# A fused two-layer transformer kernel: the first pages of its third expert run are chosen by their number and released by a count made on the chip, not sorted by a page map

## What is computed

```python
x = x + 0.5 * _L0_ffn_ref(_layernorm(x), ...)    # run 0: 8 experts of width 176, top 2, and a shared expert
x = x + _L0_attn_ref(_layernorm(x), ...)         # time shift, gates, a channel mix of 1024 hidden units
x = x + 0.5 * _L0_ffn_ref(_layernorm(x), ...)    # run 1: the weights of run 0 again
x = x + 0.5 * _L1_ffn_ref(_layernorm(x), ...)    # run 2: 32 experts of width 96, top 6, and a shared expert
x = x + _L1_attn_ref(_layernorm(x), ...)         # rotary q and k, one sum over the sequence, projection
x = x + 0.5 * _L1_ffn_ref(_layernorm(x), ...)    # run 3: the weights of run 2 again
```

```python
scores = sigmoid(x @ gate_w);  topk_w, topk_i = top_k(scores, 6);  topk_w /= sum(topk_w) + 1e-20
routed = sum over the 6 chosen experts e of  topk_w * ((silu(x @ wg[e]) * (x @ wu[e])) @ wd[e])
out    = routed + (silu(x @ sg) * (x @ su)) @ sd
```

## Time and profile before

| | us |
|---|---|
| median of 3 runs (lowest, highest) | 1299.98 (1296.2, 1301.84) |
| the profiled execution's own time | 1301.21 |
| its span, first to last instruction | 1299.4 |
| PE busy in the span | 1110.7 (85%) |
| DVE busy | 746.4 (57%) |
| ACT busy | 536.0 (41%) |
| POOL busy | 594.8 (46%) |
| third run's tile loop, PE | 712.12 to 914.06 |
| fourth run's tile loop, PE's first page | 1107.10 |

### The profile page before, as it was taken

One profiled execution on the slowest core, in us unless ns is written; L12 is line 12 of the kernel. 1 busy time (PEld: TensorE's weight loads), 2 busy tenths in 40 slices (PEclk: granted clock), 3 DMA queues, 4 the chain that ended last, 5 costly groups with the idle time before them and its releaser, 6 DMA issues. The chain is left out here.

```text
span 1299.4 us, 20577 instructions
## 1 busy us (share of the span) xinstructions
PE 1110.7 (85%) x6035; PEld 918.2 (71%) x6035; DVE 746.4 (57%) x2345; ACT 536.0 (41%) x1012; POOL 594.8 (46%) x579
## 2 busy tenths in 40 slices
PE   4899997887898999988687899999968674899994
PEld 3777775566677887766565799988545553899994
DVE  4663365645635574366645564777788655545554
ACT  3423344464533432244441344444242324466663
POOL 3580244221213233237767303667536777017776
PEclk9799998999988999999888999999888887899998
DMA  9623535920000236534353767887302232569997
GB/s 315 281 94 90 154 102 166 323 98 1 1 1 33 87 141 257 201 120 144 127 198 129 234 209 218 282 252 226 92 8 81 102 106 101 176 205 285 295 288 239
DMA packets 126073, 209.84 MB, mean 161 GB/s; under 512 B 16064, under 2 KB 105536, under 8 KB 124096
## 3 DMA queue, kind: packets, MB, share of 16 engines
q1 hardware_dynamic: 101392, 141.38, 32.8%
q0 software_dynamic: 24576, 67.14, 16.6%
HBM read 129.29 MB, written 101.19 MB: 177 GB/s over the span
## 5 line engine op out<-in xcount | busy, mean ns | idle before, releaser
L713 POOL DMA_INDIRECT G<-yd,slot_of x256 | 251.1, 981 | 297.9 <-DMA yd<-yo 216.4
L698 POOL DMA_INDIRECT xd<-xnt,slot_of x256 | 251.6, 983 | 152.4 <-issue 78.7
L982 PE MATMUL ps<-WE,xT 128*128 x1016 | 190.0, 331 | 0.6 <-issue 0.2
L2210 DVE TENSOR_TENSOR hid<-hid,ps 128x192 f32<-128x192 f32 (+2 forms) x168 | 65.3, 389 | 180.9 <-ACT hid L1624 180.6
L982 PEld LDWEIGHTS ps<-WE,xT 128*128 128x128 f32 x1016 | 164.7, 193 | 2.7 <-issue 2.6
L2189 DVE SCALAR_TENSOR_TENSOR XT<-G,wt,XT 128x256 f32<-128x256 f32 x256 | 127.6, 503 | 62.1 <-DMA G<-yd,slot_of 52.9
L1595 ACT ACTIVATE xT<-ps 128x512 f32<-128x512 f32 (+1 forms) x168 | 99.0, 589 | 140.4 <-PE ps L949 134.6
L1624 ACT ACTIVATE hid<-ps 128x192 f32<-128x192 f32 (+2 forms) x168 | 60.3, 359 | 164.3 <-PE ps L982 164.3
L949 PE MATMUL ps<-ident,xd_in 128*128 128x128 f32 x664 | 102.5, 276 | 29.7 <-DMA xd_in<-xd 20.7
L949 PEld LDWEIGHTS ps<-ident,xd_in 128*128 128x128 f32 x664 | 81.5, 142 | 42.9 <-issue 23.3
L1452 ACT ACTIVATE S<-ps 128x512 f32<-128x512 f32 (+1 forms) x72 | 42.6, 592 | 159.7 <-PE ps L887 157.4
(11 more groups left out here) (265 smaller groups left out, 2168.4 us busy)
## 6 DMA issues: line engine op xcount, KB each, us to landing
xd_in<-xd SPq DMA_DIRECT2D x140, 256.0 KB
yd<-yo SPq DMA_DIRECT2D x140, 256.0 KB, 3.2
WE<-w SPq DMA_DIRECT2D x8, 1280.0 KB, 10.2
xd_in<-xd SPq DMA_DIRECT2D x52, 128.0 KB, 2.3
yd<-yo SPq DMA_DIRECT2D x52, 128.0 KB, 2.0
W0E<-w0e SPq DMA_DIRECT2D x1, 4864.0 KB, 33.3
xd<-xnt,slot_of POOLq DMA_INDIRECT x256, 2.4
G<-yd,slot_of POOLq DMA_INDIRECT x256, 4.1
```

The lines of the kernel that those rows point to most:

```text
L698: nc.gpsimd.indirect_dma_start(xd[f // 2][:, :], bass.IndirectOffsetOnAxis(ap=slot_of[:, t, k:k + 1], axis=0), xnt[:, t, :], None).then_in ...
L713: nc.gpsimd.indirect_dma_start(G[:, n % G_RING, :], None, yd[f // 2][0:min(ly.upto[t][k], ly.TILES) * P, :], bass.IndirectOffsetOnAxis(ap= ...
L982: last = mm(dst, xT[:, q % 2, a, k, :], flat[:, bass.ds(expert[2 * q + a] + k * 2 * ly.H, 2 * ly.H)], start=(k == 0), stop=(k == KD - 1))
L2210: tt(hid[:, q % 2, 0:m, 0:ly.H], hid[:, q % 2, 0:m, 0:ly.H], src, ALU.mult).then_inc(TL.hid, 1)
```

## The change

The page map goes, with the per-page DMAs and their second semaphores, `page_order`, `omap` and the third gather in every fourth pair. Pages keep their numbers. FRONT becomes 20: after block 2 DVE still marks the whole pages, and after block 3 is ranked PE counts the whole ones ahead of each page. Partition 20 then holds how many of pages 0 to 19 are whole. If that is under 20, `more_rows` becomes 96, else 0. SP reads it into a register and waits for each of the four scatter semaphores to reach the count of blocks 0 to 2 plus this number, where 96 more stands for the 24 scatters of block 3. So the first ten pairs are loaded either as soon as blocks 0 to 2 are scattered and block 3's slots are known, or after the whole scatter. SP no longer waits for `emap`. Before pair 10 it waits for the whole scatter, as it did before pair 8. The attention weights follow the load of pair 10. Gathers wait for the pairs of `pages(t, k)` alone: 16 pairs at the least. Steps of `first_turns` are at other pairs.

```diff
-FRONT = [0, 0, 16, 0]
+FRONT = [0, 0, 20, 0]
...
-        self.upto = [[pages(t, k) for k in range(top)] for t in range(TT)]
-    def early(self, front):
-        moved = lambda n: max(n, front + min(n, self.E)) if front else n
-        return [[-(-moved(n) // 2) for n in row] for row in self.upto]
+        self.early = [[-(-pages(t, k) // 2) for k in range(top)] for t in range(TT)]
...
                 def send(q):
...
-                    if moved(q):
-                        if moved_upto(q, q % 2):
-                            wait_tile(sp, tile_sent, q, q % 2)
-                        for a, done in enumerate((TL.sent[q % Y_RING], tile_sent[q % 2][0])):
-                            sp.dma_start(yd[f // 2][bass.ds(page_at[2 * q + a], P), :], yo[:, q % Y_RING, a]).then_inc(done, 16)
-                        return
                     sp.dma_start(pairs_of(yd[f // 2])[q - q0][:, 0:m], yo[:, q % Y_RING, 0:m]).then_inc(TL.sent[q % Y_RING], 16)
-                scattered_upto(sp, GATHER0[f] + (NB - 1 if FRONT[f] else NB) * ly.NG)
                 if FRONT[f]:
-                    sp.wait_ge(RT.emap, f + 1)
+                    sp.wait_ge(RT.slots, NB * f + NB)
+                    left = sp.value_load(more_rows[FRONT[f]:FRONT[f] + 1, 0:1], min_val=0, max_val=16 * ly.NG // IN_FLIGHT)
+                    for n in range(IN_FLIGHT):
+                        sp.wait_ge(scattered[n], left + 16 * len(range(n, GATHER0[f] + (NB - 1) * ly.NG, IN_FLIGHT)))
+                else:
+                    scattered_upto(sp, GATHER0[f] + NB * ly.NG)
...
-                    if moved(q) and i % 2 == 0:
-                        next_pages(f, q)
-                    if moved(q):
...
-                        for a, done in enumerate((TL.landed[q % X_RING], tile_landed[q % 2][0])):
-                            sp.dma_start(xd_in[:, q % X_RING, a], xd[f // 2][bass.ds(page_at[2 * q + a], P), :]).then_inc(done, 16)
-                    else:
...
+                    sp.dma_start(xd_in[:, q % X_RING, 0:m], pairs_of(xd[f // 2])[i][:, 0:m]).then_inc(TL.landed[q % X_RING], 16)
...
             def attention_weights(i):
-                if i == 3:
+                if i == 10:
...
-                if t in (4, 8, 12):
-                    inverse(AT_NORM, (t - 4) // 4)
+                if t in (5, 9, 13):
+                    inverse(AT_NORM, (t - 5) // 4)
...
                 if b == NB - 1 and FRONT[f]:
-                    before(f, bank)
+                    mm(ps[:, bank, 3 * P:3 * P + 2], tri[:, :], whole_page[:, :].broadcast_to([P, 2]), start=True, stop=True)
...
                 dve.wait_ge(RT.ranked, NB * f + b + 1)
+                if b == NB - 1 and FRONT[f]:
+                    st.do(ts(more_rows[:, :], ps[:, bank, 3 * P:3 * P + 1], float(FRONT[f]), 16.0 * ly.NG / IN_FLIGHT, ALU.is_lt, ALU.mult))
...
-                    for _ in range(per_pair + (1 if FRONT[f] and (q - q0) % 4 == 3 else 0)):
+                    for _ in range(per_pair):
...
-                page_order(2, route_banks(NB - 1)[1])
```

More of the change, by code:

```diff
@@ L188, in program @@
         ecol = sb("ecol", [P, 16], F32)
-        page_map = sb("page_map", [P, P], I32)
-        emap, omap = page_map[0:1, :], page_map[32:33, :]
+        emap = sb("emap", [1, P], I32)
         whole_page = sb("whole_page", [P, 1], F32R)
-        order = sb("order", [P, 6], F32)
+        still_open = sb("still_open", [P, 1], F32)
+        more_rows = sb("more_rows", [P, 1], I32)
         wt = sb("wt", [P, TT, 8], F32)
@@ L498, in pairs_of @@
             return dram.rearrange("(n a p) d -> n p a d", a=2, p=P)
[L500 to L514, removed]
         def sent_upto(eng, n):
@@ L559, in _ @@
             sp.dma_start(WSQ[:], wsq).then_inc(wsq_in, 16)
[L561 to L569, removed]
             def tiles(f, between=None):
@@ L848, in rank @@
                 mm(ps[:, bank, (2 * NT - 1) * E:2 * NT * E], ones, half(E), start=False, stop=True).then_inc(RT.ranked, 1)
-            def before(f, bank):
-                mm(ps[:, bank, 2 * P:3 * P], ones, tri[:, :], start=True, stop=True)
-                mm(ps[:, bank, 3 * P:3 * P + 2], tri[:, :], whole_page[:, :].broadcast_to([P, 2]), start=True, stop=True)
             def expert_row(f, bank):
                 pe.wait_ge(RT.ecol, f + 1)
-                places = ident[:, :]
-                if FRONT[f]:
-                    places = eq[0][:, :, :].rearrange("p t e -> p (t e)")
-                    mm(ps[0:1, bank, 2 * P:3 * P], cvec[:, 0:1], places, start=True, stop=True)
                 if f == 3:
-                    mm(ps[0:1, bank, P:2 * P], ecol[:, 14:15], places, start=True, stop=True)
-                mm(ps[0:1, bank, 0:P], ecol[:, 13:14], places, start=True, stop=True).then_inc(RT.erow, 1)
+                    mm(ps[0:1, bank, P:2 * P], ecol[:, 14:15], ident[:, :], start=True, stop=True)
+                mm(ps[0:1, bank, 0:P], ecol[:, 13:14], ident[:, :], start=True, stop=True).then_inc(RT.erow, 1)
             def gate_up(ch, ahead):
@@ L943, in turned @@
                     pe.wait_ge(TL.landed[q % X_RING], 16 * (q // X_RING + 1))
-                    if moved(q):
-                        wait_tile(pe, tile_landed, q + 1, q % 2)
                     pe.wait_ge(TL.xT, q)
@@ L1609, in finished @@
                     if q >= Y_RING:
-                        sent_before(act, q)
+                        act.wait_ge(TL.sent[q % Y_RING], 16 * (q // Y_RING))
                     m = ly.tiles_in(q - q0)
@@ L2011, in whole_pages @@
                 st.sync()
-                st.do(ts(here, opens, cvec[:, 0:1], 0.0, ALU.is_equal, ALU.add, accum_out=order[:, 0:1]))
+                st.do(ts(here, opens, cvec[:, 0:1], 0.0, ALU.is_equal, ALU.add, accum_out=still_open[:, :]))
                 st.sync()
-                st.do(stt(whole_page[:, :], pages[:, :], cvec[:, 0:1], order[:, 0:1], ALU.is_gt, ALU.subtract))
-            def page_order(f, bank):
-                column = lambda i: order[:, i:i + 1]
-                ahead, n = ps[:, bank, 3 * P:3 * P + 1], float(FRONT[f])
-                st.sync()
-                taken, front, behind, apart_by, place = (column(i) for i in range(1, 6))
-                st.do(ts(taken, ahead, n, None, ALU.min))
-                st.do(stt(front, ahead, n, whole_page[:, :].bitcast(F32), ALU.is_lt, ALU.mult))
-                st.sync()
-                st.do(stt(behind, taken, -1.0, cvec[:, 0:1], ALU.mult, ALU.add))
-                st.sync()
-                st.do(stt(apart_by, ahead, -n, behind, ALU.add, ALU.subtract))
-                st.sync()
-                st.do(stt(place, apart_by, front, behind, ALU.mult, ALU.add))
-                st.sync()
-                ts(eq[0][:, :, :].rearrange("p t e -> p (t e)"), ps[:, bank, 2 * P:3 * P], place, n, ALU.subtract, ALU.is_equal).then_inc(RT.ecol, 1)
+                st.do(stt(whole_page[:, :], pages[:, :], cvec[:, 0:1], still_open[:, :], ALU.is_gt, ALU.subtract))
             def slots(f, b, bank):
@@ L2110, in slots @@
                         st.sync()
[L2111 to L2115 removed]
+                    ts(ecol[:, 13:14], ecol[:, 12:13], float(ly.EW), None, ALU.mult).then_inc(RT.ecol, 1)
             def experts(f, bank):
@@ L2214, in rows @@
                     if q >= Y_RING:
-                        sent_before(dve, q)
+                        dve.wait_ge(TL.sent[q % Y_RING], 16 * (q // Y_RING))
                     m = ly.tiles_in(q - q0)
@@ L2243, in tiles @@
                         weight_pair(f, n // rounds, 2 * (n % rounds))
-                    for _ in range(per_pair + (1 if FRONT[f] and (q - q0) % 4 == 3 else 0)):
+                    for _ in range(per_pair):
                         m = done[0]
-                        if m < upto * ly.NG and q - q0 >= EARLY[f][m // ly.K][m % ly.K] + after:
+                        if m < upto * ly.NG and q - q0 >= ly.early[m // ly.K][m % ly.K] + after:
                             gathered(f, m)
```

49 lines of the change are left out of this document (16 added, 33 removed).

## The result

| | before | after |
|---|---|---|
| median of 4 runs each, side by side (us) | 1299.82 | 1281.7 (1279.28 to 1284.15) |
| the profiled execution's own time | 1301.21 | 1284.15 |
| its span | 1299.4 | 1282.1 |

The ratio is 0.9864, with a 95% interval of 0.9835 to 0.9893: 18.1 us faster. The forecast was 15.7 us gained and 1284.3; the profiled execution gained 1301.21 - 1284.15 = 17.06.

The account below looks back on a forecast made before the run. PE was taken as full between pairs 11 and 42, with time to gain around that; 0.2 + 4 + 7 + 4.5 = 15.7 us off 1301.2 gave 1285.5, and 1284.3 as the median; range 1277 to 1297.

Parts of the forecast that it names:

- PE's start: Start of the third tile run: 0.2 us gained, between 0 and 0.5, from small instructions that go.
- Gated rows: Sign in the third run's late part: PE waits under 2 us for DVE's gated rows.
- The wait for pair 11: Sign at the third run's start: PE waits 2 to 3 us for pair 11's pages and for no other.
- The head: Third run's start to pair 11: later scatter wait and weights gain 4 us, bounds 0 and 7.
- The rival that the weights cost as much at pair 10 as at pair 3: Third run's start: moving the weights gains nothing there, 1288.3 us; chance 0.12.
- The late part: Third run, 838 to 914: gathers from 16 sent pairs on gain 7 us, bounds 3 and 7.8.
- first rival: Third run, 838 to 914: late waits stay, coming from work put in among the tiles; 1291.3 us, chance 0.15.
- The window: Attention to projection: eleven gathers left instead of 17 gain 4.5 us, bounds 2.8 and 7.9.
- the 6 worked out from the closing additions alone: Attention to projection: if GpSimd blocks only the rotations' closing additions, the gain is nearer 6 us.
- The count: First ten pairs: 20 of 20 pages whole, so loads pass; rival that it fails: + 9 us, 1309, chance 0.05.
- SP's queue with half as many DMAs: Third run's page transfers: one DMA per pair instead of two gains 0, PE being full with either form.
- early gathers starved nobody: Judges the rival that early gathers starve DVE throughout the third run: 5.5 us gained, 1294.5 us, chance 0.06.

Follow-up runs that it names:

- gathers_late: The changed kernel with the gathers, the inserted work and GpSimd's power operation put back where the kernel before has them; 1298.83 us.
- gathers_late_inv_moved: As gathers_late, but GpSimd's power operation stays one tile later, behind tiles 5, 9 and 13; 1288.32 us.
- weights_14: The changed kernel with the attention weights behind the load of pair 14 instead of pair 10; 1277.35 us.
- weights_14_residual_later: As weights_14, with GpSimd's residual additions of block 2 held until DVE has scaled the output weights; 1275.75 us.
- count_fails: The changed kernel with the count's comparison turned, so that 20 whole pages count as too few and SP waits for the whole scatter; 1301.88 us.
- before_inv_weights_14: The kernel before with GpSimd's power operation one tile later and the attention weights behind pair 14 instead of pair 3; 1296.4 us.

## Why the prediction was right, and which step of it failed

**The time and the side** came out as forecast (1281.7 for 1284.3, in the range), and so did most of the signs that it named. PE's start depends on the change by 0.15 us (0.2 said). The first gather is at 772.32 (near 772 said). Gated rows are waited for 0.4 us (under 2 said). The projection follows the attention by 32.7 us (34 to 35 said, so sooner than that). The wait for pair 11 was 4.17 us where 2 to 3 were said; here the head's term failed.

**The head, 4 said and 0.4 measured.** Two things went wrong in it. It was worked out to pair 11 and stopped there, though the same paragraph named "a slow clock for a pair behind it". To pair 11 the gain was 36.61 - 33.66 = 2.95 us; the slow pair then took 5.35 - 2.83 = 2.5 of it back, and that price stood nowhere in the sum. The other is the wait: 4.17 us where 2 to 3 were said. SP reached the weights 23.2 us after PE's start (732.86 - 709.65), and 22 was said, so all behind it came later; the 9 us that were taken for the weights were right (9.0 from the first issue to the last landing). This size isn't fixed: gathers_late and gathers_late_inv_moved have the same head. SP reached the weights 21.7 and 21.2 us after PE's start in them, PE waited 2.6 and 1.8 us, and it needed 36.58 and 36.19 us to pair 12, the slow pair included. The head is worth 0.4 to 3.2 us, and the profiled execution, the slowest of its four, is at the low end. The rival that the weights cost as much at pair 10 as at pair 3 was right about this execution's head. weights_14 shows that it was a matter of the place, since at pair 14 they cost nothing.

**The late part, 7 said and 9.2 measured**, above its upper bound of 7.8. The idle time vanished as said (7.26). The bound was wrong because it took PE's idle time for all there was to gain: PE's work shrank by 1.88 us as well, 1.3 of them behind the one wait of 2.12 us. The means were named without their shares: the prediction led with the early gathers, and the runs give 7.0 us to the power operation's place in GpSimd's queue and 2.8 to all the rest of the schedule, which in the trace stand behind DVE's moments. Its first rival, that the late waits come from the work put in among the tiles and not from the gathers, was thus nearer to the cause than its chance of 0.15; since the change moves that work too, the gain came anyhow.

**The window, 4.5 said and 6.4 measured.** The idle part is 4.5 (8.25 - 3.76), and 1.9 is the clock of the first key matmuls, again not in the sum. So the 4.5 for the gathers was right. PE's wait for the scaled weights fell by 7.94 - 2.34 = 5.6, and 1.1 us of that appears as a longer wait for ACT ahead (1.43, before 0.31; it is 0.31 again in weights_14_residual_later, so the lock makes it). Within the window the lock cost 3.1 us, in instructions with two SBUF inputs alone. That the total of 6.4 is near the 6 worked out from the closing additions alone is luck: it left out the four gathered rows (2.0 us), and the clock made up for them.

**The remaining steps.** The count holds (count_fails); its failing was priced at 9 us over the kernel before and costs 2, as PE needs 31.20 us to pair 11 where 33 were said and the late part and the window give 14.0 where 11.5 were said. SP's queue with half as many DMAs was costed at nothing because "PE was full with either form". That is true while the ring is full; after a hold it isn't, as before_inv_weights_14 shows. What was saved ahead of the projection reached the end whole (153.93 and 153.89), and early gathers starved nobody.

The total was closer than its terms, which is luck: 3.6 us too much in the head, 2.2 and 1.9 too little behind it, and 2.3 us of spread ahead of the change, less 1.2 behind it.

## What to carry to other kernels

Price a wait of PE twice: the idle time, and what runs behind it at the lower clock (here 2.5 us for one pair, 1.9 us for sixteen matmuls). The second price is a range that starts at 0: behind the same wait of 2.1 us the clock fell in three kernels and stayed at 1.00 in three others, and behind waits of 2.77 and 2.83 us the next pair took 2.85 us in one kernel and 4.33 in another. A bound from idle time alone is too low for what removing a wait can give. Work put in among the tiles is best kept off the last pair, which is a short one. In an engine's queue written out by hand, look for a small instruction that waits and at what stands behind it, since its place by one tile was worth 7 us and its cost was booked under another engine's name. Before a large load is moved in a queue, ask how full the ring is there: right behind a hold it is empty, and four pairs later it covers 2.2 MB where SP issues two DMAs to a pair.

## What the runs showed that was not expected

The issue time of plain DMAs on SP's queue, about 0.45 us each, doesn't show while a ring is full, and it decides how fast the ring fills again: four DMAs to a pair, with the page numbers read every other pair, leave 0.2 to 0.7 us of 2.825 to catch up with, two leave over 1.5. And gains in different parts don't add where one engine's queue has no slack: in the kernel before 2.7 us won at the head were gone at the first power operation, while in the kernel after, whose gathers start 26 us earlier, the 6.6 us of weights_14's head (39.01 - 32.39, two traces) were lost in no later part.
